# A four-layer graph network on one core: GpSimd's wait for TensorE in mid-step gives way to a wait for its own gathers

## The reference

```
x = layernorm(x + L0(x));  x = layernorm(x + L1(x));  x = layernorm(x + L2(x));  x = layernorm(x + L3(x))

L0:  xw = x @ W;  ew = edge_attr @ edge_w            # edge_attr: 206250 x 16
     msg = xw[src] * ew                              # one gathered row for each edge
     out = segment_sum(msg, dst) + b
L1:  agg = segment_sum(x[src], dst) / max(deg, 1);   out = agg @ W_l.T + b_l + x @ W_r.T
L2:  the same sum with 1/sqrt(degree) on both sides, then a product with weight, and bias
L3:  the same kind of sum of x @ gcn_w, tanh, a sigmoid gate, relu, batch norm over the nodes
```

## Time and profile before

| | |
|---|---|
| median of three runs | 2831.36 us (2830.82 to 2834.81) |
| span of the profiled execution, first to last instruction | 3281.4 us |
| its edge loop, first to last gather (L722) | 32.4 us to 2521 us |
| from the last gather to the end | 760.4 us |
| GpSimd in these two parts | 1550.8 us and 97.6 us busy |
| TensorE in these two parts | 1605.2 us and 704.9 us busy |

### The profile page before, as it was taken

One profiled execution on the slowest core, in us unless ns is written; L12 is line 12 of the kernel. 1 busy time (PEld: TensorE's weight loads), 2 busy tenths in 40 slices (PEclk: granted clock), 3 DMA queues, 4 the chain that ended last, 5 costly groups with the idle time before them and its releaser, 6 DMA issues.

```text
span 3281.4 us, 35388 instructions
## 1 busy us (share of the span) xinstructions
PE 2326.1 (71%) x13074; PEld 1466.3 (45%) x13074; DVE 1559.3 (48%) x2576; ACT 497.8 (15%) x798; POOL 1652.8 (50%) x1762
## 2 busy tenths in 40 slices
PE   3566656666666666667666567666677989999996
PEld 2344444444444444444444344444444544455553
DVE  2555554555554555555555555555554531222126
ACT  1011111111111111111111111111111221111113
POOL 5566656656666666656666656656664110002212
PEclk6556556566666776777777777777777999999998
DMA  6223232323333343433344344444445988876661
GB/s 203 57 86 87 82 88 84 106 84 92 107 96 99 101 122 95 120 100 110 113 135 114 106 116 121 136 121 132 119 128 120 245 294 306 291 268 247 248 242 40
DMA packets 456700, 456.22 MB, mean 139 GB/s; under 512 B 163573, under 2 KB 402250, under 8 KB 456522
## 3 DMA queue, kind: packets, MB, share of 16 engines
q1 hardware_dynamic: 237358, 281.24, 25.7%
q0 software_dynamic: 52832, 109.16, 12.5%
q10 hardware_dynamic: 166332, 63.48, 8.0%
HBM read 368.61 MB, written 85.13 MB: 138 GB/s over the span
## 4 chain that ended last, share of the span: by engine, by line
another core or an unknown queue 46%; PE 35%; ACT 7%; issue 7%; DVE 2%; DMA 2%; SPq 0%; ACTq 0%; POOL 0%; DVEq 0%; POOLq 0%
PE pb L1509 8%; PE pb L1510 8%; ACT tmp L1636 7%; PE pb L1378 5%; PE pb L1405 4%; PE pb L1368 2%; PE pb L1384 2%; PE pb L1326 2%; PE pb L1437 2%; PE pb L1527 1%; DMA big<-at 1%; DMA tmp<-at 0%; ACTq L1642 0%; ACT big L1670 0%
## 5 line engine op out<-in xcount | busy, mean ns | idle before, releaser
L722 POOL DMA_INDIRECT big<-xw,big x1612 | 1527.1, 947 | 954.7 <-issue 580.0
L909 DVE TENSOR_TENSOR big<-pb,big 128x512 f32<-128x512 f32 x404 | 260.0, 685 | 1073.1 <-remote 683.2
L1378 PE MATMUL pb<-big 128*128 128x98 f16 x3136 | 272.9, 248 | 643.2 <-ACT tmp L1636 562.1
L1405 PEld LDWEIGHTS pb<-big 128*128 128x128 f32 x3232 | 546.2, 258 | 349.1 <-issue 334.1
L1405 PE MATMUL pb<-big 128*128 128x64 f32 x3232 | 584.1, 346 | 124.4 <-issue 119.6
L1636 ACT CAST tmp<-pb 128x784 f16<-128x784 f32 x392 | 318.3, 812 | 2043.0 <-remote 1628.5
L1378 PEld LDWEIGHTS pb<-big 128*128 128x128 f16 x3136 | 231.9, 124 | 726.5 <-issue 405.6
L835 DVE TENSOR_TENSOR big<-pb,big 128x2048 f16<-128x2048 f32 x196 | 447.5, 2283 | 0.8
L1326 PE MATMUL pb<-big 64*128 64x512 f32 x808 | 327.3, 898 | 108.4 <-DVE big L909 83.7
L837 DVE TENSOR_TENSOR big<-pb,big 128x1568 f16<-128x1568 f32 x196 | 348.8, 1780 | 0.0
L1384 PE MATMUL pb<-tmp,ident 128*128 128x392 f16 x784 | 239.1, 446 | 0.0
(11 more groups left out here) (231 smaller groups left out, 1600.0 us busy)
## 6 DMA issues: line engine op xcount, KB each, us to landing
at<-tmp SPq DMA_DIRECT2D x196, 392.0 KB
big<-at SPq DMA_DIRECT2D x24, 3200.0 KB, 10.9
big<-at SPq DMA_DIRECT2D x24, 3072.0 KB, 19.7
big<-at ACTq DMA_DIRECT2D x32, 896.0 KB
big<-xw,big POOLq DMA_INDIRECT x1612
big<-in_ea SPq DMA_DIRECT2D x202, 64.0 KB
big<-at SPq DMA_DIRECT2D x13, 896.0 KB
big<-at ACTq DMA_DIRECT2D x24, 336.0 KB
```

The costliest lines, as they stand in the source:

```text
L722: nc.gpsimd.indirect_dma_start(gath[:, T8 * (n % NG) + t % T8, :], None, xw_d, bass.IndirectOffsetOnAxis(ap=src_i[:, t:t + 1], axis=0)).th ...
L909: nc.vector.tensor_tensor(msg[:, T8 * (n % 2) + 4 * q:T8 * (n % 2) + 4 * q + 4, :], PB[:, q, :].rearrange("p (t f) -> p t f", f=D), gath[: ...
L1378: last = nc.tensor.matmul(PB[:, 4 + g, i * KW:i * KW + KW], hot_lo[:, at_pair, :], hot_key[:, at_pair, :], start=True, stop=True)
L1405: last = nc.tensor.matmul(PB[:, 2 + n % 2, 0:WIN], msg[:, T8 * (n % 2) + t, :], hot_win[:, T8 * (n % 2) + t, :], start=(t == 0), stop=(t = ...
```

## The change

GpSimd's wait in mid-step (lines 718 to 721) is taken out. Instead, ahead of the first gather of each step n from 1 on, GpSimd waits until all eight gathers of step n-1 have landed. The wait for VectorE's reading of the slot stays where it was, behind the new one.

```diff
             for n in range(NH):
-                if n >= NG:
-                    pool.wait_ge(s_msg, 2 * (n - NG) + 2)
+                if n >= 1:
+                    pool.wait_ge(s_gath[(n - 1) % NG], 16 * T8 * ((n - 1) // NG + 1))
+                    if n >= NG:
+                        pool.wait_ge(s_msg, 2 * (n - NG) + 2)
                     pool.sem_inc(s_seen, 1)
                 for t in range(n * T8, min(n * T8 + T8, ET)):
-                    if t % T8 == T8 // 2 and n >= LAG + 2:
-                        pool.wait_ge(s_pe, n)
-                        pool.wait_ge(s_amm, 2 * (n - LAG - 1))
-                        pool.sem_inc(s_seen, 1)
                     nc.gpsimd.indirect_dma_start(gath[:, T8 * (n % NG) + t % T8, :], None, xw_d, ...
```

## The result

The changed kernel takes **3418.9 us** (median of 4 runs, 3411.2 to 3424.5), the kernel before, run beside it, 2832.7 us (2830.8 to 2834.8): ratio 1.206, 95% interval 1.204 to 1.209. The change costs 586 us. Forecast were 3188 us, between 3070 and 3260: the right side, but the cost 1.6 times as large as the 357 us of the sum.

The account below looks back on a forecast made before the run. GpSimd's gather issuing was taken to bound the edge loop in plain runs, with no waiting. Removing the mid-step wait gains nothing and the added wait costs 340 + 17 = 357 us: 2831 to 3188 us, range 3070 to 3260.

Parts of the forecast that it names:

- 357 us of the sum: Added wait in the edge loop: 176 steps at 1.93 us plus 25 with a slot fetch at 0.68 us.
- 439 us of waiting: GpSimd's real waiting in the profiled edge loop, mostly in mid-step; claimed absent from the plain runs.
- TensorE's late signals: Mid-step in the trace: TensorE's signal held back while GpSimd issues, out 2.7 us after GpSimd falls silent.
- something about the trace must block: Claim that tracing holds the kernel back, since trace and plain runs differ by 450 us.
- 32.4 + 2049 + 760.4 = 2842 us: Head, edge-loop gathers without any wait, and rest; claimed to match the plain runs' median of 2831 us.
- 3281 - 439 + 357 = 3199: Forecast span in us of the changed kernel's profiled execution: old waiting removed, new wait's cost added.
- 1.93 us a step: Added wait at a step's start: 1.5 to the landing plus 0.73 restart less the 0.30 gap.
- I take 1.5, near the two undisturbed ones: Time from the last gather's issue end to its landing, put at 1.5 us, ends 1.0 and 3.3.
- third landing, of 3.3 us: Last gather of step 118 as VectorE sees it; held for a bad step, not the mean.
- Rival D: Landings meet table loads: 91 loads each delay one by 1.8 us, adding 164 us, 3350 us; chance 0.04.
- The restart: From the end of GpSimd's added wait to its next gather: 0.73 us.
- Rivals A, B, C: A: trace's waits real, 2749 us, chance 0.06; B: faster gathers, 2943 us, 0.07; C: TensorE's signal stuck, 3450 us, 0.03.

Follow-up runs that it names:

- e1_no_wait: The kernel before without its mid-step wait, and without the wait the change added: 2834.3 us, ratio 1.0004 to the kernel before.
- e4_both: The changed kernel with the mid-step wait for TensorE put back, so both waits: 3426.7 us, ratio 1.2096 to the kernel before.
- e6_traffic_moved: The changed kernel with SyncE's store and ScalarE's load of table blocks held until gathers have landed: 3248.1 us, ratio 1.147 to the kernel before.
- e7_store_twice: The changed kernel with each store of a table block made twice, the second into an unread table: 3577.6 us, ratio 1.264 to the kernel before.
- e5_twice: The changed kernel with a second wait in mid-step, for the same step's first four gathers to land: 3726.0 us, ratio 1.315 to the kernel before.
- e8_before_again: The kernel before, unchanged, profiled a second time: a single run of 2836.9 us, profiled span 2835.1 us.
- e2_two_back: The changed kernel, but GpSimd waits ahead of step n for the gathers of step n-2: 2834.5 us, ratio 1.0001 to the kernel before.

## Why the prediction was wrong

**The bound: right, though one reason for it was false.** GpSimd's issuing alone fills the time of the plain runs. Leaving the mid-step wait out (e1_no_wait) or putting it back (e4_both) changes nothing, and in the second profile of before the loop runs from 32 to 2082 us with no waiting. I had taken the 439 us of waiting for an effect of tracing, and the prediction leaned on TensorE's late signals for it. The changed kernel's trace has its signals on time, and so has the second trace of before; that first execution was odd, and what held it is open. The prediction's sentence that something about the trace must block isn't borne out. The comparison that carried the step was the plainer one, 32.4 + 2049 + 760.4 = 2842 us against a median of 2831; with the 753 us that follow the loop in the second profile it is 2834 us, against a span of 2835.1. For the same reason "3281 - 439 + 357 = 3199" for the changed kernel's span was right only in taking the 439 us out: it is 3422 us, 580 more than the 2842 that would be left.

**The added wait: mechanism right, the landing mis-sized.** One pause ahead of each step, 0.30 us everywhere else, all other engines waiting for gathers: all as said. The cost was put at 1.93 us a step and is 3.11 (3.41 - 0.30). The failing step is "I take 1.5, near the two undisturbed ones". It measured 2.46 us in the mean (1.96 to the last packet, 0.50 to the end of the wait), 0.96 us more, 176 x 0.96 = 169 us. Undisturbed the value was good: 1.21 + 0.39 = 1.60 us in e6_traffic_moved. The landings that gave 1.0 to 1.64 us had no other traffic beside them; in step 114 the store was issued 4.6 us before the gather's issue ended and the next one behind the landing. The third landing, of 3.3 us, was set aside as a bad step, though the trace of before shows what stood beside it (traffic at the quiet landing of step 114, then at that of step 118):

```profile
1453.00:1453.50 0.50, 0.00 (x0) 0.00 (x0) 0.00 (x0) 0.00 (x0) 0.50 (x1) 1.00 0.51 123
...
1514.75:1515.50 0.75, 0.75 (x5) 0.75 (x5) 0.75 (x2) 0.00 (x0) 0.45 (x1) 0.50 1.15 394
1515.50:1516.00 0.50, 0.50 (x5) 0.50 (x4) 0.50 (x1) 0.00 (x0) 0.50 (x1) 0.50 0.98 339
```

In the changed kernel the wait fixes the order of things: a landing starts a step of VectorE, TensorE and ScalarE, and their store and loads come some 8.5 us later, when GpSimd's last gather of the next step goes out. The store is issued 1.8 us before the end of that issue in the median and in no step behind it; in the second trace of before it lies anywhere from 3 us before to 1.5 us behind in nine steps of ten. Of 176 landings 143 meet other traffic, about half of these only 50 to 200 KB of it. e6_traffic_moved (171 us less) and e7_store_twice (159 us more) show it from both sides. Rival D had the mechanism in part, with a chance of 0.04: it counted ScalarE's 91 loads and left out SyncE's 196 stores. That its 164 us come near the measured 169 is luck, since it put 1.8 us on 91 landings, where 143 take 1.2 us more than the quiet ones. It should have been part of the sum.

**The restart: nearly right.** 0.73 us in most steps, but 2.35 us in 23 of them, every eighth step, so 0.95 us in the mean; 176 x 0.22 = 39 us. Why every eighth is open; in the traces of the changed kernel, e4_both, e5_twice, e6_traffic_moved and e7_store_twice it is the same 2.35 us in the same 23 steps, so it hangs on the place in GpSimd's sequence and not on the traffic, and where no wait holds (e1_no_wait, e8_before_again) no such gap appears. The remainder is in the 25 steps with a fetch of slots: 2.09 us each and not 0.68, 35 us, since their landing is disturbed as well. 357 + 169 + 39 + 35 = 600 us, against 599 in the trace.

**Rivals A, B, C** fell: no run holds mid-step waiting, the pace is 1.25 us in every trace, and no signal of TensorE is late. The Trainium skill's figure ("DMA: Bandwidth & Descriptors", anatomy of one DMA on GpSimd's path), by which the time would have been 3127 us, agrees with the undisturbed landing up to its last packet, 0.95 + 1.21 us from the start of the issue against its 2.15; GpSimd's wait is over 0.39 us after that. The figure says nothing of the disturbed one.

## What to carry to other kernels

Where one engine's issuing bounds a loop, a wait for its own last transfer costs the whole latency each time, and a wait that is reached a few issues later costs little or nothing: here 586, 82 and 4 us with 0, 2 and 4 issues in between. Such a wait also locks the phases of the queues, so its latency has to be taken beside the traffic that will stand there, not from a quiet landing. And when a profiled execution is 16% longer than the runs, hold its sum of issues against the runs before believing its waits; here the second profile of the same kernel had none of them.

## What the hardware showed beside that

- In one profiled execution of before the updates of TensorE's semaphores are recorded more than 8 us behind the ends that the trace gives its matmuls, while GpSimd issued gathers (1544.9 against 1536.6 us in the earlier trace rows). The profiler models these ends, so how late the updates were is known only as far as that. This was seen in one of the two profiles of that kernel and in none of the nine profiles of other kernels.
- A wait that is over when it is reached leaves GpSimd's gap at 0.30 us and the time unchanged (e2_two_back); behind a wait that holds the next gather starts 0.73 us after the wait is over, and 2.35 us after it in every eighth step.
- A gather of 128 rows of 512 bytes has landed 1.2 us after its issue ended on quiet queues, and 3.8 us after it in the 18 steps where other queues moved 0.9 MB or more meanwhile.
